# A planner of attention's maxima with three banks in every step, and lambda's chain in four parts

## The reference

```python
q = (x @ Wq.T).reshape(b, t, 2 * H, D)          # 16 sub-heads of 8
k = (x @ Wk.T).reshape(b, t, 2 * H, D)
v = (x @ Wv.T).reshape(b, t, H, 2 * D)
q = _apply_rope(q, freqs, scale); k = _apply_rope(k, freqs, 1.0 / scale)
scores = jnp.einsum('bhtd,bhsd->bhts', q * scaling, k)
probs = jax.nn.softmax(scores, axis=-1)
lam = exp(sum(lambda_q1 * lambda_k1)) - exp(sum(lambda_q2 * lambda_k2)) + LAMBDA_INIT
diff = probs[:, :, 0] - lam * probs[:, :, 1]
attn = jnp.einsum('bhts,bhsd->bhtd', diff, v)
attn = attn * rsqrt(mean(attn * attn, axis=-1) + 1e-05) * (1.0 - LAMBDA_INIT)
...
zone_outputs = zone_outputs + (gelu(x @ Wa[e]) @ Wb[e]) * w[:, e]   # 3 of 8 experts for each batch row
...
x = x + attention(xn) + ffn(xn)                  # xn: the layer norm of x
```

## Time and profile before

| what | value |
|---|---|
| three executions | 429.24, 429.36 and 430.72 us, median 429.36 |
| the profiled execution | 429.37 us, of which the trace's span is 427.6 |
| TensorE (PE) busy | 412.2 us, 96% of the span |
| VectorE (DVE) busy | 383.8 us, 90% |
| ScalarE (ACT) busy | 344.1 us, 80% |
| GpSimd (POOL) busy | 146.1 us, 34% |
| granted TensorE clock | 1.00 of full speed |

### The profile page before, as it was taken

How to read it: one execution, slowest core, us unless ns; L and a number is a source line. 1 busy time by engine, 2 the same in 40 slices (tenths; PEclk the granted TensorE clock), 3 DMA queues, 4 the chain that set the end, 5 groups by cost and what they waited for, 6 DMA issues and landing times.

```text
span 427.6 us, 7728 instructions
## 1 busy us (share of the span) xinstructions
PE 412.2 (96%) x2750; PEld 191.0 (45%) x2750; DVE 383.8 (90%) x737; ACT 344.1 (80%) x459; POOL 146.1 (34%) x179
## 2 busy tenths in 40 slices
PE   8998999999999999999999999999999999999996
PEld 6664566566665333333333333333333333335544
DVE  4989999999999899999999999999999999888575
ACT  2787765675654799889899989989999999989993
POOL 4159998988863500111020110120103303420000
PEclk9999999999999999999999999999999999999999
DMA  9726760400000060020002054000000000000003
GB/s 268 304 92 208 264 231 22 138 13 1 3 0 2 16 233 2 4 98 4 2 1 101 1 129 71 3 2 2 3 2 2 3 0 3 2 3 2 2 2 100
DMA packets 21872, 24.95 MB, mean 58 GB/s; under 512 B 11818, under 2 KB 16106, under 8 KB 21578
## 3 DMA queue, kind: packets, MB, share of 16 engines
q1 hardware_dynamic: 21096, 23.60, 17.5%
q10 hardware_dynamic: 738, 0.86, 0.8%
HBM read 14.49 MB, written 8.65 MB: 54 GB/s over the span
## 4 chain that ended last, share of the span: by engine, by line
PE 74%; DVE 11%; ACT 7%; issue 5%; DMA 1%; POOL 1%; ACTq 0%
PE ps L1395 21%; PE ps L1358 16%; PE ps L1248 13%; ACT E L809 6%; DVE part_max L924 6%; PE ps L1320 4%; PE ps L1173 3%; PE ps L1175 3%; PE ps L1174 3%; PE ps L1386 3%; PE ps L1321 2%; PE ps L1322 2%; PE ps L1376 2%; DMA X<-in_x 1%; PE ps L1350 1%
## 5 line engine op out<-in xcount | busy, mean ns | idle before, releaser
L924 DVE TENSOR_REDUCE part_max<-ps 128x1 f32<-128x512 f32 x512 | 320.6, 681 | 21.9 <-PE ps L1248 15.0
L809 ACT ACTIVATE E<-ps 128x1024 f32<-128x1024 f32 x256 | 245.3, 1029 | 29.3 <-PE ps L1358 25.9
L1395 PE MATMUL ps<-E,Vg 128*32 128x512 f32 x896 | 119.3, 604 | 0.0
L1248 PE MATMUL ps<-K,Q 32*128 32x512 f32 x384 | 104.2, 463 | 1.4 <-DVE part_max L924 1.1
L1358 PE MATMUL ps<-Q,K 32*128 32x512 f32 x320 | 70.8, 489 | 2.1 <-ACT E L809 1.4
L559 POOL TENSOR_TENSOR hL<-h,hH 128x512 fp32r<-128x512 f32 x48 | 61.4, 1288 | 13.1 <-ACT hH L769 11.2
L1358 PEld LDWEIGHTS ps<-Q,K 32*128 32x128 f32 x320 | 28.6, 181 | 82.7 <-ACT E L809 72.3
L767 ACT ACTIVATE h<-ps 128x512 f32<-128x512 f32 x48 | 28.8, 601 | 33.6 <-PE ps L1175 25.1
L1248 PEld LDWEIGHTS ps<-K,Q 32*128 32x128 f32 x384 | 44.4, 182 | 23.9 <-DVE part_max L924 19.3
L610 POOL TENSOR_TENSOR U<-AT,rsum 128x256 f32<-128x256 f32 x15 | 9.3, 623 | 102.4 <-DVE rsum L1060 102.4
L1248 PE MATMUL ps<-xnL,xnH 32*128 32x512 f32 x128 | 41.8, 454 | 0.9 <-DVE part_max L924 0.7
(11 more groups left out here) (171 smaller groups left out, 418.0 us busy)
## 6 DMA issues: line engine op xcount, KB each, us to landing
K<-k_scr SPq DMA_DIRECT2D x5, 512.0 KB, 3.8
Q<-q_scr SPq DMA_DIRECT2D x5, 512.0 KB, 7.1
tab<-in_tables SPq DMA_DIRECT2D x2, 1024.0 KB, 10.0
wa_raw<-in_wa SPq DMA_DIRECT2D x6, 256.0 KB, 2.9
wb_raw<-in_wb SPq DMA_DIRECT2D x6, 256.0 KB, 3.2
Q<-max_turned SPq DMA_DIRECT2D x80, 2.0 KB
X<-in_x SPq DMA_DIRECT2D x2, 512.0 KB, 7.0
k_scr<-V SPq DMA_DIRECT2D x2, 512.0 KB, 10.9
```

Of the source, the lines that this page charges most:

```text
L809: nc.scalar.activation(E[:, par, 2 * jj:2 * jj + 2, :].rearrange("p j t -> p (j t)"), ps[:, 2 * jj:2 * jj + 2, :].rearrange("p j t -> p (j ...
L924: nc.vector.tensor_reduce(part_max[:, tile // FC % 2, j * FC + tile % FC, sh:sh + 1], ps[:, SLOT_BANK[x], :], AX.X, ALU.max).then_inc(slot ...
L1248: mm(ps[:, SLOT_BANK[x], :], Qs[g % KQ_BUFS][strip(j), tile % TB * P:(tile % TB + 1) * P], Ks[g % KQ_BUFS][strip(j), sh * BANK:(sh + 1) * ...
L1395: last = mm(ps[QUAD * j:QUAD * (j + 1), B_PV, :], Vg[:, par, st, j // 2, :], E[:, s % 2, k, :], start=(st == 0), stop=(st == TB - 1), skip ...
```

## The change

`max_slots` gives every step of attention three slots (the first one four, as before): the old function gave 3.06 on average up to step 97 and 2.78 after. Five steps lose their fourth slot (16, 32, 49, 65 and 81) and five that had two get a third (102, 107, 111, 116 and 120); from step 81 to step 101 the count is five slots behind the old one, and equal again behind step 120. `lambdas` is cut in four parts of three operations, which stand behind the slots of steps 13, 29, 45 and 61 on VectorE.

```diff
-MAX_STEPS, PACE_STEPS = 121, 98
+MAX_STEPS = 121
...
 def max_slots(s):
 
-    own = GJ * 2 * TB
 
     def up_to(n):
-        if n <= PACE_STEPS:
-            return GJ * LEAD - (-n * (GJ * (QUADS - LEAD) - own) // PACE_STEPS)
-        return GJ * QUADS - own + min(own, -(-(n - PACE_STEPS) * own // (MAX_STEPS - PACE_STEPS)))
+        return min(GJ * LEAD + (3 * n + 1 if n else 0), GJ * QUADS)
     return [divmod(x, 4) for x in range(up_to(s), up_to(s + 1))]
...
+LAMBDA_AT = (13, 29, 45, 61)
...
-            lambdas()
             for n in range(UNITS):
                 for t, k in lead_slots(n):
                     reduce_slot(t, k)
...
+            def lambdas(part):
+                nl, ab, cc, c2, nlc = (lt[:, k:k + 1] for k in range(5))
+                if part == 0:
+                    dve.wait_ge(lam_exp, 1)
...
                 if s >= TB and s % TB < 3:
                     query_rows(s // TB - 1, (s // TB - 1) % 2, s % TB)
+                if s in LAMBDA_AT:
+                    lambdas(LAMBDA_AT.index(s))
                 if s in SUMS_AT:
                     sums_turn(SUMS_AT.index(s))
```

More of the change, by code:

```diff
@@ L1048, in _ @@
                     rotary(EARLY // 2, (n - (UNITS - 2),))
+            def lambdas(part):
+                nl, ab, cc, c2, nlc = (lt[:, k:k + 1] for k in range(5))
+                if part == 0:
+                    dve.wait_ge(lam_exp, 1)
+                    link(nc.vector.scalar_tensor_tensor(nl, lam_e[:, 1:2], LAMBDA_INIT, lam_e[:, 0:1],
+                                                        ALU.subtract, ALU.subtract))
+                    link(nc.vector.tensor_scalar(ab, nl, -1.0, None, ALU.mult))
+                    link(nc.vector.tensor_tensor(ab, ab, nl, ALU.max))
+                elif part == 1:
+                    link(nc.vector.tensor_scalar(ab, ab, 1.0, None, ALU.add))
+                    link(nc.vector.reciprocal(cc, ab))
+                    link(nc.vector.tensor_scalar(cc, cc, LAMBDA_RANGE, 1.0, ALU.mult, ALU.min))
+                elif part == 2:
+                    link(nc.vector.tensor_tensor(c2, cc, cc, ALU.mult))
+                    link(nc.vector.tensor_scalar(epsc[:], c2, EPS, SQRT_LEAST, ALU.mult, ALU.max))
+                    link(nc.vector.tensor_scalar(limit[:], c2, FLT_MAX, None, ALU.mult))
+                else:
+                    link(nc.vector.tensor_tensor(nlc, nl, cc, ALU.mult))
+                    link(nc.vector.tensor_scalar(comb[:], cst[:, C_E0:C_E0 + 2 * QUAD], cc, None, ALU.mult))
+                    nc.vector.scalar_tensor_tensor(comb[:], cst[:, C_E1:C_E1 + 2 * QUAD], nlc, comb[:],
+                                                   ALU.mult, ALU.add).then_inc(comb_done, 1)
             def query_rows(a, th, part):
```

## The result

| what | before | after |
|---|---|---|
| median, 20 executions of each | 430.59 us | 433.14 us |
| lowest and highest | 429.24 and 432.00 | 430.69 and 435.69 |
| the profiled execution, and its span | 429.37, 427.6 | 433.34, 431.1 |
| granted clock of the profiled execution | 1.00 | 0.992 |

The ratio is 1.0057, with a 95% interval of 1.0042 to 1.0073: the change costs 2.45 us (1.8 to 3.1). The forecast was 429.6 (427.1 to 431.9) and no change; the time lies outside the range, and the kernel is slower by a little over half a per cent.

What follows compares the result with a forecast made beforehand. It took TensorE, VectorE and ScalarE to be loaded alike in attention, with the last-ending wait deciding each stage. Terms -1.0 - 3.0 + 1.2 + 1.0 + 2.0 = +0.2 us gave 429.6 us, no change, range 427.1 to 431.9.

Steps and rivals of the forecast that it cites:

- A: Expert stage: without lambda's chain TensorE's wait near 42 us goes, -1.0 us (bounds -0.9 to -1.75).
- B: Attention steps 16, 32, 49, 65, 81: four-bank steps become three-bank steps, -3.0 us (bounds -2.5 to -3.35).
- C: Attention behind steps 13, 29, 45, 61: lambda's 12 VectorE operations come back, +1.2 us (bounds 0 to 2.6).
- D: Attention steps 102, 107, 111, 116, 120: two-bank steps become three-bank steps, +1.0 us (bounds 0.35 to 3.2).
- E: Step 103: half 13's maxima are turned later, so TensorE waits for their rows, +2.0 us (bounds 0.9 to 3.3).
- the hole is paid back: Rival: steps after 103 return the wait's time; 427.1 us, or 427.9 with A at 1.0; chance 0.22.
- VectorE as the bound: Rival: in attention each bank costs its reduction wherever it stands and lambda its whole 2.6 us; 433.0 us, chance 0.13.
- GpSimd's lock: Rival: GpSimd's exclusion of two-input VectorE operations follows lambda's chain into attention; 431.5 us, chance 0.05.
- the expert stage did gain: Answers the rival that GpSimd's queue bounds 40 to 56 us, so A is 0; 430.6 us, chance 0.10.

Runs made afterwards that it cites:

- 1: Kernel before with only lambda's chain moved in four parts behind steps 13, 29, 45 and 61, old slots: 431.05 us against 430.58, ratio 1.0006.
- experiment 6: Whole change with half 13 turned two slots earlier (hole of about 1 us): 430.29 us against 430.31 before, ratio 0.9992.
- experiment 9: Whole change, half 13 turned early, lambda behind steps 12, 52, 60, 84, and half 12 turned late (hole at step 96): 432.65 us against 429.92 before, 1.0057.
- 2: Kernel before with only the new max_slots, lambda's chain left in the expert stage: 432.29 us against 430.58, ratio 1.0052.
- experiment 4: Kernel before with only half 13 turned five slots later, where the change puts it: 433.46 us against 430.58, ratio 1.006.
- experiment 3: Whole change with half 13 turned three slots earlier: 429.70 us against 430.58 before, ratio 0.9974.
- experiment 5: Whole change with the hole filled by nine unused products of K with itself on TensorE: 431.49 us against 430.31 before, ratio 1.0011.
- 8: Kernel before with the new max_slots and half 13 turned early, lambda in the expert stage: 429.27 us against 430.31, ratio 0.9973.
- 10: Kernel before with half 13 turned late and the hole filled by nine unused products: 432.38 us against 429.92, ratio 1.0044.

## Why the prediction was wrong

The terms, each from the rows of the table that differ in it alone:

| term | forecast | measured | from |
|---|---|---|---|
| A, lambda leaves the expert stage | -1.0 | -1.1 | first copy, 157.91 (mean of 1, 6, 9) against 158.97 (mean of before, 2, 4) |
| B, five four-bank steps go | -3.0 | -2.74 | 11 windows, 2 against before |
| C, lambda in attention | +1.2 | +1.3 to +1.45 | 1 against before; after and 3 against 2 |
| D, five two-bank steps get a third | +1.0 | +1.2 | 3 windows, 3 against before |
| E, the hole at step 103 | +2.0 | +1.9 | 3 windows, 5 against 3; 4 against before +1.85 |
| the clock behind the hole | 0 | +1.3, up to +1.85 | 3 windows, after and 2 against 5; by the ratios of after and 5, 2.0 |

**The step that failed is E's price.** "I take 2.3 ..., and give back 0.3 ...: +2.0 us" counts the wait and stops there. The wait is what I said it was, in its place, cause and length (2.17 us), but an idle TensorE was not the end of it: 0.3 us behind it the clock fell to 1.2 GHz for 3.41 us in the profiled execution, and that is another 1.3 us. The mean clocks say that this is the usual case: 0.992 or less in 19 of 20 executions, and below 0.994 in none of the 12 with the hole filled. Experiment 5 shows the cause by taking the idleness away and leaving the wait; experiment 9 shows it at another hole.

The five terms alone make +0.6 (-1.1 - 2.7 + 1.3 + 1.2 + 1.9), and experiment 5, which has these five and no lower clock behind the hole, stands at +0.5 (-0.3 to +1.3). The whole change stands at +2.45, so over all executions the lower clock cost about 2.0 us, more than the 1.3 of the profiled one. The mean clock, a rough count, agrees: it is on average 0.0091 below full after the change and 0.0033 in experiment 5, a difference of about one and a half stretches of 0.004. Stretches of twice the length, as in experiments 2 and 9, would account for it; how many executions after the change had one was not seen.

**The base was the second error.** I set the sum on a profiled execution at full clock all through. By the mean clock two thirds of the executions of the kernel before are not (23 of 34), and 430.6 was the time to start from. From there the forecast's own sum gives 430.8, inside the range, so the base alone doesn't explain the miss; the measured terms with the clock behind the hole give 430.6 + 1.9 = 432.5, or 433.1 with the longer stretch.

**A** held in its working: the loss of 1.75 us at 42 us is gone, and GpSimd's queue takes back 0.8 of it at 53 and 55 us (2.37 + 2.49 - 2 x 2.02); the 1.08 us that I had read as the room at the tightest place is about what was kept. **B** was 0.26 too much. **C** had the operations right (0.13 to 0.29 us each, 2.05 in all instead of 2.6) and the share too low: 1.4 of the 2.05 us reached the end, about 0.7 of them, where I had taken a share of 0.45; too many microseconds and too low a share offset each other, so that C came out near by luck. In the single windows it spread thin, and the longest of the eleven took 17.37 us. **D** was 0.2 too little, in part since even the early turn of experiment 3 leaves a wait of 0.25 us. (The upper bounds add up to +5.7, not to the +5.75 that the prediction states.)

**The rivals.** That the hole is paid back is refuted: experiments 4 and 9 keep 1.85 and 4.1 us to the end. VectorE as the bound would have made D 3.2 us, which cost 1.2, and the loss goes in experiment 3 with VectorE's work unchanged. Its 433.0 us stands beside the measured 433.14 by luck. GpSimd's lock didn't follow the chain (no operation of it took over 0.29 us), and the expert stage did gain.

## What to carry over

When a change delays a wait of TensorE, price the wait and what comes behind it: a hole of 2 us in a stream of matmuls cost 3.2 in the profiled execution of the change, and 1.85 in that of experiment 4, where the clock stayed full. A table that says how much work stands in each step also sets when everything that hangs on its last piece is ready; move that piece's own trigger (here three slots) along with the table, and the same change is a gain. Take a base from enough executions to know which clock the profiled one had.

## What was new about the hardware

- Around the end of an idle hole of 2.14 to 2.17 us TensorE's granted clock fell to 0.50, for 3.41 us (after) or about 6.8 us (experiments 2 and 9). It fell 0.6 us ahead of the first matmul behind the hole in experiment 9, 0.3 us behind it after the change and 1.3 us behind it in experiment 2. Behind a hole of 2.25 us it stayed at 1.00 once (experiment 4), and behind one of 0.96 us it stayed there too. The Trainium skill (TensorE: Matmul & The Clock Gate, Part 1) says of the start of a kernel that the number of slow matmuls differs between executions of the same kernel. No run here shows that for the start; over the whole kernel the mean clock of the 20 executions after the change ran from 0.983 to 1.00, and here the difference is as large as the effect of an edit.
- Nine products that nobody reads, 2.33 us of TensorE's time in a hole, saved 1.28 us in the profiled execution: they cost nothing, since TensorE was waiting anyway.
- Stretches of 3.41 us at 0.50 also come at places with no hole of that length ahead: at 28.79 after the change, in the middle of matmuls of the projections and 2.2 us behind a wait of 0.53 us, and in five other profiled executions behind waits of 0.2 to 0.9 us. They cost 0.9 to 1.4 us each. In experiments 8 and 10 they came 1.3 to 2.4 us behind TensorE's wait of 0.7 us for lambda's chain, but 0.96 us of waiting in experiment 6 brought none in its profiled execution; what brings them was not found.
